# A two-layer decoder on one core: new orders in the first cross attention and the Performer, and part of the four-bit rounding of h on GpSimd

## What is computed

```
x = x + L0_attn(ln(x))        # stage A: windowed attention, 16 heads of 64
x = x + L0_xattn(ln(x), ctx)  # stage B: cross attention, softmax over the 32 best of 154 scores
x = x + L0_ffn(ln(x))         # stage C: w_down(silu(gate) * up), inputs and weights rounded to four bits
x = x + L1_attn(ln(x))        # stage D: Performer, 6 layers
x = x + L1_xattn(ln(x), ctx)  # stage E: cross attention, 16 heads of 8
x = x + L1_ffn(ln(x))         # stage F: 6 layers of windowed attention and feed-forward

def fp4_quant_dequant(x):     # blocks of 16
    scale = max(max|x| / 6, 1e-12)
    return grid[nearest(|x| / scale)] * sign(x) * scale

def performer_layer(out):     # each of the 6 layers of stage D
    q, k, v = out @ Wq + bq, out @ Wk + bk, out @ Wv + bv
    Qp, Kp = exp(+-q @ omega - |q|^2 / 2), exp(+-k @ omega - |k|^2 / 2)
    a = causal_linear_attention(Qp, Kp, v)     # num / (den + 1e-6), chunks of 128 tokens
    h1 = layer_norm(out + a @ Wo + bo) * g1 + be1
    return layer_norm(h1 + relu(h1 @ W1 + bf1) @ W2 + bf2) * g2 + be2
```

## Time and profile before

| | |
|---|---|
| three timed runs | 1661.90, 1667.17, 1668.22 us; median 1667.17 us |
| the profiled execution | 1669.83 us by the device, 1667.9 us from its first to its last instruction |
| mean granted TensorE clock | 0.959 of full speed |
| busy | PE 1531.1 us (92%), DVE 1170.8 (70%), ACT 922.0 (55%), POOL 623.8 (37%) |
| chain that ended last | PE 65%, DVE 16%, ACT 11%, issue 4%, DMA 2%, POOL 2% |
| DMA queue | 116.99 MB, 21.5% of the 16 engines' time |

### The profile page before, as it was taken

How to read it: one execution, slowest core, us unless ns; L and a number is a source line. 1 busy time by engine, 2 the same in 40 slices (tenths; PEclk the granted TensorE clock), 3 DMA queues, 4 the chain that set the end, 5 groups by cost and what they waited for, 6 DMA issues and landing times.

```text
span 1667.9 us, 37573 instructions
## 1 busy us (share of the span) xinstructions
PE 1531.1 (92%) x15357; PEld 788.0 (47%) x15357; DVE 1170.8 (70%) x2014; ACT 922.0 (55%) x1626; POOL 623.8 (37%) x578
## 2 busy tenths in 40 slices
PE   7787668999999999889999999999999999999996
PEld 2545434545555554333535455453545545363543
DVE  5786575657666665346777878687787877778783
ACT  2435432453445344345667767666776767676673
POOL 5462000010001000104565656555564655556461
PEclk9899677999999999889999999999999999999998
DMA  7143210000000000203142423313242331324120
GB/s 244 41 129 137 95 27 1 8 22 1 22 6 17 22 1 1 97 1 117 22 133 68 138 86 90 129 36 132 69 137 73 103 125 40 125 77 137 57 82 14
DMA packets 52393, 119.38 MB, mean 72 GB/s; under 512 B 15488, under 2 KB 20352, under 8 KB 50816
## 3 DMA queue, kind: packets, MB, share of 16 engines
q1 hardware_dynamic: 52224, 116.99, 21.5%
HBM read 37.52 MB, written 0.52 MB: 23 GB/s over the span
## 4 chain that ended last, share of the span: by engine, by line
PE 65%; DVE 16%; ACT 11%; issue 4%; DMA 2%; POOL 2%; SPq 0%; DVEq 0%; ACTq 0%; POOLq 0%
PE ps L436 5%; PE ps L426 5%; PE ps L292 4%; PE ps L274 4%; PE ps L390 3%; PE ps L284 3%; PE ps L1699 3%; PE ps L407 3%; PE ps L1645 3%; PE ps L1703 2%; ACT big L558 2%; PE ps L1665 2%; DVE nm L676 2%; DVE big L628 2%; ACT big L570 2%
## 5 line engine op out<-in xcount | busy, mean ns | idle before, releaser
L727 POOL TENSOR_TENSOR big<-big 128x512 f32<-128x512 f32 x112 | 144.2, 1288 | 282.3 <-DMA big<-big 281.8
L736 POOL TENSOR_TENSOR big<-big,nm 128x384 f32<-128x384 f32 x224 | 185.1, 847 | 157.0 <-DVE nm L669 157.0
L627 DVE TENSOR_TENSOR big<-ps,big 128x512 f32<-128x512 f32 x224 | 153.8, 686 | 65.9 <-ACT sq L504 40.6
L2059 POOL TENSOR_TENSOR big<-big 128x512 f32<-128x512 f32 x24 | 31.2, 1324 | 415.7 <-ACT big L1834 415.7
L1973 DVE TENSOR_TENSOR big<-ps,fix 128x512 f32<-128x512 f32 x192 | 119.2, 683 | 55.3 <-PE ps L1645 54.9
L558 ACT ACTIVATE big<-big 128x384 f32<-128x384 f32 x224 | 109.3, 523 | 86.3 <-DVE big L679 84.1
L628 DVE TENSOR_TENSOR big<-ps,big 128x512 f32<-128x512 f32 x224 | 152.5, 681 | 0.0
L728 POOL TENSOR_TENSOR big<-big 128x512 f32<-128x512 f32 x112 | 146.2, 1305 | 0.0
L426 PE MATMUL ps<-big 128*64 128x64 f32 x3584 | 131.2, 227 | 12.8 <-ACT big L570 12.8
L426 PEld LDWEIGHTS ps<-big 128*64 128x64 f32 x3584 | 116.6, 140 | 52.7 <-ACT big L570 34.5
L676 DVE TENSOR_REDUCE nm<-ps 128x4 f32<-128x384 f32 x224 | 112.5, 544 | 30.4 <-PE ps L390 27.8
(11 more groups left out here) (307 smaller groups left out, 2833.1 us busy)
## 6 DMA issues: line engine op xcount, KB each, us to landing
big<-big SPq DMA_DIRECT2D x224, 256.0 KB, 2.4
big<-big SPq DMA_DIRECT2D x112, 128.0 KB, 2.4
big<-in_F_w SPq DMA_DIRECT2D x18, 512.0 KB, 4.0
big<-in_zero SPq DMA_DIRECT2D x8, 1088.0 KB, 12.6
big<-big SPq DMA_DIRECT2D x84, 64.0 KB, 2.0
big<-in_D_w SPq DMA_DIRECT2D x12, 256.0 KB, 3.1
big<-in_F_wo SPq DMA_DIRECT2D x6, 512.0 KB, 3.7
big<-in_F_w SPq DMA_DIRECT2D x6, 341.0 KB, 3.3
```

Of the source, the lines that this page charges most:

```text
L627: dve.tensor_tensor(tmp[:, i, w, :], ps[:, k, :], tb[:, 2 * w, :], ALU.mult).then_inc(*part.mark((key, b, p, 0)))
L736: pool.tensor_tensor(v, v, nm[:, p % 3, 16 + 4 * h:20 + 4 * h].unsqueeze(2).to_broadcast([128, 4, KW]), ALU.mult)\
```

## The change

It has four parts. (1) In stage B the transposes and copies of the rounded weights leave the tile loop and go into stage C, one third each between the steps of the normalization of the second entry; they use banks 4, 5, 6 in place of 0, 1, 5. (2) In stage B the end of the first entry is written in another order: `b_inv_act(0)` stands right behind the copy of tile 3, `b_norm_dve(0)` behind the search of tile 6, `b_out_pe(0)` ahead of the values of tile 6, and DVE adds to `x` after all eight searches. (3) The last three steps of the rounding of h go to POOL for tiles 2 and 3 of entry 0 and for tile 3 of entry 1; DVE does the other five tiles. DVE waits for POOL's part of entry 0 before it rounds entry 1, PE before it transposes a tile of POOL's. (4) In stage D PE issues the q, k and v products of the next unit before the last chunk of the numerator of this one; DVE's order follows, and the product for `Om` (`d_om_dve`) moves into the next unit.

```diff
         def b_pe(pe):
...
-            for n in range(TILES + 1):
-                if n == TILES - 2:
+            for n in range(TILES):
+                if n == TILES - 1:
                     b_out_pe(pe, 0)
-                if n == TILES - 1:
+                    b_values_pe(pe, n - 1)
                     norm_mean_pe(pe, "C1", 0, 4, x[:, cols(0)], (x_new.at(("B", 0)),))
-                if n < TILES:
-                    b_turn_pe(pe, n)
+                b_turn_pe(pe, n)
...
-                if n == TILES:
-                    norm_var_pe(pe, "C1", 0, 4)
-                if n > 0:
+                if 0 < n < TILES - 1:
                     b_values_pe(pe, n - 1)
-                if n == NT:
-                    c_w_pe(pe)
+            norm_var_pe(pe, "C1", 0, 4)
+            b_values_pe(pe, TILES - 1)
...
         def b_act(act):
...
-                if n > 0:
+                if 0 < n < TILES - 1:
                     b_turn_act(act, n - 1)
                 if n == NT:
-                    c_w_act(act)
+                    b_inv_act(act, 0)
+            norm_sq_act(act, "C1", 0, 4)
+            b_turn_act(act, TILES - 1)
...
         def b_dve(dve):
...
-                if n == TILES - 3:
+                if n == TILES - 2:
                     b_norm_dve(dve, 0)
-                if n == TILES - 2:
-                    out_dve(dve, "B", 0, Bb[:, 3:4], B_Y[0])
+            out_dve(dve, "B", 0, Bb[:, 3:4], B_Y[0])
...
         def c_pe(pe):
-            norm_pe(pe, "C1", 1, 7, x[:, cols(1)], (x_new.at(("B", 1)),))
+            c_w_pe(pe, 0)
+            norm_mean_pe(pe, "C1", 1, 7, x[:, cols(1)], (x_new.at(("B", 1)),))
+            c_w_pe(pe, 1)
+            norm_var_pe(pe, "C1", 1, 7)
+            c_w_pe(pe, 2)
...
+                    if t == H_DVE[b]:
+                        pe.wait_ge(*q4_pool.at(b))
...
+        H_DVE = (2, 3)
+
+        def h_part(b, pool):
+            tiles = slice(H_DVE[b], NT) if pool else slice(0, H_DVE[b])
...
         def c_hq_dve(dve, b):
...
+            if b > 0:
+                dve.wait_ge(*q4_pool.at(b - 1))
+            step(dve, dve_step, fp4_scale(dve, v, nb, qb))
+            step(dve, dve_step, dve.tensor_tensor(blocks_of(qa, NT * I0), v, wide(qb[:, 1, :], nb), ALU.mult))
+            step(dve, dve_step, dve.tensor_scalar(qu.bitcast(I32), qa.bitcast(I32), EXPONENT, None, ALU.bitwise_and))
+            dve.tensor_scalar(qu, qu, 1.0, ROUND, ALU.max, ALU.mult).then_inc(*q4_unit.mark(b))
+            dve.wait_ge(*q4_unit.at(b))
+            a_, u_, h_, scale = h_part(b, False)
+            step(dve, dve_step, dve.tensor_tensor(a_, a_, u_, ALU.add))
+            step(dve, dve_step, dve.tensor_tensor(a_, a_, u_, ALU.subtract))
+            dve.tensor_tensor(h_, a_, scale, ALU.mult).then_inc(*q4.mark(("h", b)))
             dve.wait_ge(*q4.at(("h", b)))
+
+        def c_pool(pool):
+            for b in range(B):
+                pool.wait_ge(*q4_unit.at(b))
+                a_, u_, h_, scale = h_part(b, True)
+                step(pool, pool_step, pool.tensor_tensor(a_, a_, u_, ALU.add))
+                step(pool, pool_step, pool.tensor_tensor(a_, a_, u_, ALU.subtract))
+                pool.tensor_tensor(h_, a_, scale, ALU.mult).then_inc(*q4_pool.mark(b))
...
         def d_pe_half(pe, h):
-            hd, tl = head_of(h), tail_of(h)
-            if hd:
+            hd, tl, nx = head_of(h), tail_of(h), head_of(h + 1)
+            if h == 0:
                 d_qk_pe(pe, *hd)
+                d_v_pe(pe, *hd)
...
+            d_den_pe(pe, *hd)
+            if nx:
+                d_qk_pe(pe, *nx)
+                d_v_pe(pe, *nx)
+            d_num_pe(pe, *hd, 3)
...
         def d_dve_half(dve, h):
             hd, tl = head_of(h), tail_of(h)
+            d_qk_dve(dve, *hd)
+            d_v_dve(dve, *hd)
             if tl:
                 d_a_dve(dve, *tl)
-            if hd:
-                d_qk_dve(dve, *hd)
+            if hd[1] == 0 and hd[0] > 0:
+                d_om_dve(dve, hd[0])
```

More of the change, by code:

```diff
@@ L1018, in b_act @@
             norm_act(act, "B1", 1, 7, 0)
-            for n in range(TILES + 1):
-                if n == NT + 1:
-                    b_inv_act(act, 0)
-                if n == TILES - 2:
+            for n in range(TILES):
+                if n == TILES - 1:
                     b_bias_act(act, 0)
-                if n < TILES:
-                    b_exp_act(act, n)
-                else:
-                    norm_sq_act(act, "C1", 0, 4)
+                    b_turn_act(act, n - 1)
+                b_exp_act(act, n)
                 if n == 0:
@@ L1125, in w_back_dve @@
             dve.tensor_tensor(Cw, Wv(), wide(wb[:, 0, :], 70), ALU.mult).then_inc(*q4_w.mark("w"))
-        C_W = (0, 1, 5)
-        def c_w_pe(pe):
-            pe.wait_ge(*q4_w.at("w"))
-            for j, off in enumerate((0, 24, 48)):
-                k = C_W[j]
-                take(pe, k)
-                for ch in range(3):
-                    m = min(128, I0 - 128 * ch)
-                    if j < 2:
-                        last = pe.transpose(ps[:, k, 128 * ch:128 * ch + m],
-                                            Cw[0:m, off + 8 * ch:off + 8 * ch + 8, :].rearrange("p a b -> p (a b)"), ident[0:m, 0:m])
-                    else:
-                        last = pe.transpose(ps[0:m, k, 128 * ch:128 * ch + 128],
-                                            Cw[:, off + 8 * ch:off + 8 * ch + m // FB, :].rearrange("p a b -> p (a b)"), ident[:, :])
-                last.then_inc(*full[k].mark(("C", "w", j)))
@@ L1144, in c_w_act @@
-        def c_w_act(act):
-            for j, dst in enumerate((gT, uT)):
-                act.wait_ge(*full[j].at(("C", "w", j)))
-                act.activation(dst, ps[:, j, 0:I0], ACT.Copy).then_inc(*turned4.mark(("w", j)))
-                read(act, j, turned4, ("w", j))
-            act.wait_ge(*full[C_W[2]].at(("C", "w", 2)))
-            step(act, act_step, act.activation(dT[:, 0:2, :], ps[:, C_W[2], 0:256].rearrange("p (a b) -> p a b", a=2), ACT.Copy))
-            act.activation(dT[0:96, 2, :], ps[0:96, C_W[2], 256:384], ACT.Copy).then_inc(*turned4.mark(("w", 2)))
-            read(act, C_W[2], turned4, ("w", 2))
+        C_W = (4, 5, 6)
@@ new lines, in build, with c_w_pe @@
+        q4_unit, q4_pool = sg("q4_unit"), sg("q4_pool")
+        def c_w_pe(pe, j):
+            off, k = 24 * j, C_W[j]
+            if j == 0:
+                pe.wait_ge(*q4_w.at("w"))
+            take(pe, k)
+            for ch in range(3):
+                m = min(128, I0 - 128 * ch)
+                if j < 2:
+                    last = pe.transpose(ps[:, k, 128 * ch:128 * ch + m],
+                                        Cw[0:m, off + 8 * ch:off + 8 * ch + 8, :].rearrange("p a b -> p (a b)"), ident[0:m, 0:m])
+                else:
+                    last = pe.transpose(ps[0:m, k, 128 * ch:128 * ch + 128],
+                                        Cw[:, off + 8 * ch:off + 8 * ch + m // FB, :].rearrange("p a b -> p (a b)"), ident[:, :])
+            last.then_inc(*full[k].mark(("C", "w", j)))
@@ new lines, in c_w_act @@
+        def c_w_act(act, j):
+            k = C_W[j]
+            act.wait_ge(*full[k].at(("C", "w", j)))
+            if j < 2:
+                act.activation((gT, uT)[j], ps[:, k, 0:I0], ACT.Copy).then_inc(*turned4.mark(("w", j)))
+            else:
+                step(act, act_step, act.activation(dT[:, 0:2, :], ps[:, k, 0:256].rearrange("p (a b) -> p a b", a=2), ACT.Copy))
+                act.activation(dT[0:96, 2, :], ps[0:96, k, 256:384], ACT.Copy).then_inc(*turned4.mark(("w", 2)))
+            read(act, k, turned4, ("w", j))
@@ L1211, in c_act @@
         def c_act(act):
-            norm_act(act, "C1", 1, 7, 0)
+            c_w_act(act, 0)
+            norm_sq_act(act, "C1", 1, 7)
+            c_w_act(act, 1)
+            norm_root_act(act, "C1", 1, 7, 0)
+            c_w_act(act, 2)
             for b in range(B):
@@ L1749, in d_pe_half @@
                 d0_mean_pe(pe)
-            if hd:
-                d_v_pe(pe, *hd)
-                d_phi_pe(pe, *hd, 1)
+            d_phi_pe(pe, *hd, 1)
             if tl:
                 d_var1_pe(pe, *tl)
-            if hd:
-                d_phi_pe(pe, *hd, 0)
-                d_kt_pe(pe, *hd)
-            if not tl:
-                d0_var_pe(pe)
+            d_phi_pe(pe, *hd, 0)
+            d_kt_pe(pe, *hd)
             if tl:
```

82 lines of the change are left out of this document (38 added, 44 removed).

## The result

The changed kernel takes 1654.76 us in the median of five timed runs (1654.02 to 1657.6), beside 1667.17 for the kernel before: ratio 0.9941, 95% interval 0.9923 to 0.9959, that is 6.4 to 12.8 us less. Timed again later beside 18 runs of before, it had 0.9939 (0.992 to 0.9959). The profiled execution took 1657.6 us by the device, with a span of 1655.7 in place of 1667.9. The forecast was 1654.5. The total fits; its terms do not, and the rest of the document is about that.

A forecast was written before the change was run, and what follows sets the result against it. PE was taken to bound stage D, an engine-to-engine chain the end of B and C. Terms -6.4 (D), -3.3 (B), -3.1 (C) sum to -12.8 us, forecasting 1654.5 us, own range 1651 to 1658, wider range 1647 to 1662.

The forecast's parts named there:

- D, -6.4 forecast: Stage D: PE's 0.64 us wait for the masks vanishes at ten boundaries, -6.4 us, bounds -7.0 and -4.
- 2.7 us of work where 0.64 us of waiting was: Stage D, chunk 3: q, k (1.82 us) and v (0.9) between denominator and numerator cover the wait for masks.
- 0 to 0.1: Stage D: PE's remaining wait for `d_norm` before the output projection's second product, 0 to 0.1 us.
- B, -3.3 forecast: End of stage B: inversion starts 2.6 us earlier, first rounding step at 196.3 against 199.60, -3.3 us; bounds -2.0 and -8.
- rival (c): Stages B to D, clock moves: full clock gives B 4.5 us more, total 1647 to 1650; chance 0.10 good, 0.08 bad.
- The B stretch runs at half clock: End of stage B: claimed at half clock although PE is busy for 10 us on end.
- the 2.6 of the earlier start: Stage B: ACT's inversion of the denominator starts at 176.9 instead of 179.48, right behind tile 3's values, -2.6 us.
- C, -3.1 forecast: Stage C: POOL's share of rounding h saves 2.0 us in the first part, -3.1 us together; bounds -3.3 and +0.6.
- POOL all but stands still while DVE does that: Stage C: beside DVE additions with both operands in SBUF, POOL loses 2.4 of 2.8 us in the first rounding.
- One of the prediction's own signs of being wrong: Stages B to D: the prediction counts as wrong if the clock there differs by more than 0.03.
- Rival (d): Stage D, L1612: `o` comes later than 325.1, PE stands in front of q, time 1676; chance 0.04.
- rival (b): Stage C: POOL is late, so the stage gives nothing or costs 0.6 us, time 1658.2; chance 0.08.

The follow-up runs named there:

- e2: Kernel before with only stage B's new order and the move of the weights' transposes into stage C: 1660.79 us, ratio 0.9965.
- e8: Changed kernel with h rounded on DVE alone, denominator ahead of third numerator, v between the output projection's two products: 1674.0 us, ratio 1.0041 to before.
- e11: Kernel before with only the weights' transposes and copies moved from stage B into stage C: 1662.49 us, ratio 0.9979.

## Why the forecast's total held and its terms did not

- **D, -6.4 forecast: mis-sized.** The wait went as said and nothing new waits at L1612. "2.7 us of work where 0.64 us of waiting was" priced the products themselves rightly (1.82 and 0.98), but not what their place does to the neighbours: the denominator now stands ahead of a product of full width, the projection between tiled ones. The unit gives 0.34 in place of 0.64. The "0 to 0.1" for `d_norm` is at most a part of that: the projection is 0.11 longer where the bias product does not cover it. Ten times 0.34 is 3.4, outside the bounds of -7.0 and -4. The window's 4.9 has 1.5 more from its first and its last unit (0.7 and 0.8), which the sum had at nothing: v left the last one for the one before, and the first, which has one more v, took 0.7 less at a granted clock of 0.89 in place of 0.84. The new neighbours had no term in the sum at all.
- **B, -3.3 forecast: right in its mechanism.** With the clock raised late it is 3.3 to 3.4 (19.3 and 19.5 us in e2 and e8). In after, 1.8 of the 4.5 of rival (c)'s good side came on top: 5.1. "The B stretch runs at half clock" was read too simply: before has 0.72 there, with the full clock from 178.5 to 182.0, 188.8 to 192.2 and 195.6 to 199.0, but PE's long pieces lie between these. The weights' transposes alone gave 3.0 over B's end and C in e11, as against the 2.6 of the earlier start.
- **C, -3.1 forecast: wrong in sign, 0.6 us lost on DVE.** The step that failed is "POOL all but stands still while DVE does that". In the earlier trace rows DVE's instruction had started first, at 116.33, and POOL's at 116.49; I read a rank of engines out of an order of starts. The prices of POOL alone were near (1.70 and 1.55 forecast, 1.69 and 1.39 measured). With steps of both engines issued back to back, each waits for the other in turn and DVE pays for POOL's: in the first rounding two of its steps take 1.35 more each, 2.7 us, where narrower steps save 2.2; in the second twice 0.61, where they save 1.1.
- **Sum.** D too large by 1.5 and C by 4.1; B too small by 1.8, and 3.2 from stages that nobody touched in that one profile. That the errors cancelled is luck: the total is no evidence for the terms. One of the prediction's own signs of being wrong was there to see: the clock differs by 0.05 in the end of B (0.77 for 0.72) and in D's first unit, where it allowed 0.03. Rival (d), `o` late, did not appear; rival (b)'s result came (C gives nothing), by another mechanism.

## What to carry to other kernels

Split work between VectorE and GpSimd only where VectorE's own instructions are of a kind that GpSimd doesn't hold up: here, those with a PSUM operand and reductions; side by side, on two SBUF operands each, the two take turns, and sharing gained nothing. When a wait on TensorE is filled with work from elsewhere, price the work by the neighbours it will have, and move the consumer's program on every other engine along with it. And read a total that fits term by term: the unit of D and the rounding on DVE each have a stretch of their own that repeats to hundredths, while single runs of one kernel differ by up to 10 us.

## What the runs showed of the hardware

- A VectorE instruction with two SBUF operands and a GpSimd addition exclude one another, and the second to start waits: 64 columns took 1.57 and 1.70 us in place of 0.22. Beside a GpSimd instruction with one operand VectorE lost only 0.45 us, once in four. Of GpSimd's 1.69 us for 704 columns about 1.35 are held against VectorE (an estimate: 2.24 - 0.89).
- A VectorE instruction with a single SBUF operand of 1408 columns in 0.89 us is held too; a reduction of the same 1408 columns in 1.62 us is not.
- Products on TensorE of full width that follow or precede tiled ones cost 0.08 to 0.12 us more from start to start, and so does the tiled denominator ahead of one of full width (1.01 for 0.91); which property of the pair costs it was not taken apart.
- With the same program for stage B the granted clock went from 1.2 to 2.4 GHz 8.1 us behind the values of tile 3 in after and 11.2 and 11.5 us behind them in e2 and e8, and the stretch took 17.7, 19.3 and 19.5 us: when it rises is worth 1.7 us there.
